# A decoder layer on one core: scores inside the recurrence from streamed per-head keys, and per-head values for the attention tail

## The reference

```python
# sLSTM stack (4 layers, 4 heads of 32), a scan over time
raw = wx_t + einsum('bhd,hdgo->bhgo', h, rk) + b
lfm = m + log_sigmoid(fr); mn = maximum(ir, lfm)
ig = exp(ir - mn); fg = exp(lfm - mn)
cn = fg * c + ig * tanh(zr); nn = fg * n + ig
hn = sigmoid(og) * cn / nn
# cross-attention, 16 heads of 64, context ctx_768 of 6404 x 96
q = (x @ Wq), k = (context @ Wk), v = (context @ Wv), split by head
attn = softmax(q @ k.T / sqrt(64)); out = (attn @ v) @ Wo + bo
# experts: top-1 routing with capacity, relu MLP 128 -> 512 -> 128
```

## Time and profile before

| | us |
|---|---|
| median of three runs | 4382.3 (4378.4 to 4395.1) |
| the profiled execution | 4380.9 |
| its span, first to last instruction | 4379.1 |
| plain chunks (320 steps) | 768.4 |
| 64 steps before the first tile | 181.8 |
| 832 steps with a tile | 2172.0 |
| tail, 816 tiles | 1026.0 |
| TensorE busy, of the span | 3756.0 (86%) |
| VectorE, ScalarE, GpSimd busy | 3519.7, 2778.4, 1036.2 |

### The profile page before, as it was taken

How to read it: one execution, slowest core, us unless ns; L and a number is a source line. 1 busy time by engine, 2 the same in 40 slices (tenths; PEclk the granted TensorE clock), 3 DMA queues, 4 the chain that set the end, 5 groups by cost and what they waited for, 6 DMA issues and landing times. The chain is left out here.

```text
span 4379.1 us, 103876 instructions
## 1 busy us (share of the span) xinstructions
PE 3756.0 (86%) x37640; PEld 2172.9 (50%) x37640; DVE 3519.7 (80%) x15928; ACT 2778.4 (63%) x8992; POOL 1036.2 (24%) x1218
## 2 busy tenths in 40 slices
PE   4666666459999999999999999999969999999997
PEld 3433334335445444544544544454426666666666
DVE  7777777688888888888888888888668787887875
ACT  4555555435666666666666666666717778877784
POOL 1000000000000000000000000000018888888883
PEclk6555555558999999999999999999969999999999
DMA  3111111000000000000000000000031221221100
GB/s 89 36 42 38 40 43 35 8 4 2 2 5 2 2 4 3 3 4 3 2 2 4 2 2 2 3 2 2 3 90 24 47 47 26 46 47 39 33 9 25
DMA packets 62974, 90.36 MB, mean 21 GB/s; under 512 B 11095, under 2 KB 58007, under 8 KB 59351
## 3 DMA queue, kind: packets, MB, share of 16 engines
q1 hardware_dynamic: 59282, 79.35, 7.3%
q10 hardware_dynamic: 3176, 4.36, 0.4%
HBM read 53.63 MB, written 28.83 MB: 19 GB/s over the span
## 5 line engine op out<-in xcount | busy, mean ns | idle before, releaser
L1214 PEld LDWEIGHTS G<-st,rec_w 128*128 128x128 f16 x19456 | 605.5, 99 | 961.3 <-DVE st L1385 926.5
L1214 PE MATMUL G<-st,rec_w 128*128 128x1 f16 x19456 | 683.0, 165 | 407.4 <-DVE st L1385 390.4
L1644 POOL TENSOR_TENSOR plt<-pft,pht 128x512 f16<-128x512 f32 x765 | 865.5, 1159 | 213.4 <-ACT pft L1639 110.5
L1166 PE MATMUL OA<-pf,vals 128*97 128x512 f32 (+1 forms) x1632 | 849.1, 601 | 0.6
L1089 ACT ACTIVATE st<-hb 32x16 f16<-32x16 f32 x1216 | 259.0, 213 | 703.0 <-DVE hb L1380 702.4
L130 DVE TENSOR_REDUCE mx<-MT 128x1 f32<-128x512 f32 (+1 forms) x832 | 531.7, 665 | 101.2 <-PE MT L1693 92.1
L1069 ACT ACTIVATE pf<-SC,ln_prob 128x512 f32<-128x512 f32 (+1 forms) x816 | 560.5, 687 | 20.6
L130 DVE TENSOR_REDUCE mx<-MB 128x1 f32<-128x512 f32 (+1 forms) x832 | 537.5, 660 | 37.7 <-PE MB L122 22.8
L1639 ACT ACTIVATE pft<-ST,ln_prob 128x512 f32<-128x512 f32 (+1 forms) x816 | 536.5, 684 | 36.0 <-PE ST L1715 30.9
L1637 ACT ACTIVATE pht<-ST,ln_prob 128x512 f16<-128x512 f32 x510 | 350.4, 687 | 241.8 <-PE ST L1715 235.7
L1080 ACT ACTIVATE tf<-G 32x16 f32<-32x16 f32 x1216 | 211.8, 174 | 384.6 <-PE G L1214 356.9
(11 more groups left out here) (354 smaller groups left out, 6774.2 us busy)
## 6 DMA issues: line engine op xcount, KB each, us to landing
kc<-scr_k SPq DMA_DIRECT2D x32, 816.0 KB, 13.1
scr_k<-k_hl SPq DMA_DIRECT2D x192, 128.0 KB, 1.7
k<-scr_k SPq DMA_DIRECT2D x16, 816.0 KB, 6.7
w<-in_L_ffn_W SPq DMA_DIRECT2D x16, 256.0 KB, 4.5
xin<-x SPq DMA_DIRECT2D x38, 48.0 KB, 1.8
scr_k<-k_hl SPq DMA_DIRECT2D x16, 96.0 KB, 1.6
rnat<-in_L_attn_rker SPq DMA_DIRECT2D x3, 256.0 KB, 13.8
up_w<-in_L_attn_ff_up SPq DMA_DIRECT2D x1, 672.0 KB
```

The source lines that it names most:

```text
L1166: pe.matmul(OA[0:at.DC + 1, :], at.vals[0:rows, i, :], pf[0:rows, tile % 2, :], start=(i == 0), stop=(i == KT - 1)).then_inc(pv_done, 1)
L1214: mm = pe.matmul(g[:, t, c:c + 1], rec_w[:, c, :], st[:, c:c + 1], start=False, stop=(c == C - 1), skip_group_check=True)
L1644: return eng.tensor_tensor(pl[0:k, t % NP_, :], pf[0:k, t % NP_, :], ph[0:k, t % NP_, :], ALU.subtract)
```

## The change

**Scores in tiled steps** use the same per-head form as the tail. Per tile and head two matmuls of 128 columns, eight in all, take the place of three of 512. Their keys no longer lie in SBUF: SP loads groups of four tiles by four heads from `scr_k` into a ring of three (`kc_in`: high and low part stacked to 128 rows; `k2_in`: high part and the row of ones), three DMAs a group, 208 groups. A group's buffer is refilled when the last tile of the group three before is done; loads that would fall on t = 15 to 19 are put off to t = 20. The queries for it (`pe_head_queries`, four matmuls with `wq_d`) are made three steps after the queries for the maxima, which remain; ScalarE copies them in two halves and VectorE takes the residue two steps later.

**Plain chunks** now also compute the values V = context times Wv by head, 102 pieces of one tile by eight heads, each again three matmuls of 512 columns, a copy and a residue. Pieces have 21 positions in a chunk; stores of up to four tiles by eight heads (1 MB) go to `scr_v`. The positions 22 and 24 of the weight preparation become 24 and 26. The split of `vals_c` is gone.

**The tail** loads `vc`, the per-head values, from `scr_v` and uses 129 and 65 columns instead of 193 and 97; the output is then multiplied by `wo_sb`. Loads of values for head g + 2 wait for the last product of head g.

Tensors used only in the plain chunks are freed after them; the two rings take their place, and two tensors of the setup share memory with `pf`.

```diff
-def pe_scores(pe, at, bank, j, unit, k):
-    keys = slice(j * P, j * P + k)
-    pe.matmul(bank[0:k, :], at.keys_l[:, keys], at.qh[0:DC, unit, :], start=True, stop=False)
-    pe.matmul(bank[0:k, :], at.keys_h[0:DC, keys], at.ql[:, unit, :], start=False, stop=False)
-    return pe.matmul(bank[0:k, :], at.keys_h[:, keys], at.qh[:, unit, :], start=False, stop=True)
+def pe_scores(pe, at, bank, j, unit, kept, k):
+    first = j % at.GROUP * P
+    for i in range(at.HEADS_A_UNIT):
+        cols = slice(i * P, (i + 1) * P)
+        pe.matmul(bank[0:k, cols], at.kc_in[:, kept, i, first:first + k], at.qd_in[:, unit, cols], start=(i == 0), stop=False,
+                  skip_group_check=True)
+        mm = pe.matmul(bank[0:k, cols], at.k2_in[:, kept, i, first:first + k], at.q2_in[:, unit, cols], start=False,
+                       stop=True, skip_group_check=True)
+    return mm
...
+def pe_head_queries(pe, at, bank, unit):
+    for i in range(at.HEADS_A_UNIT):
+        mm = pe.matmul(bank[:, i * P:(i + 1) * P], at.wq_d[:, unit * at.HEADS_A_UNIT + i, :], at.xat[:, :], start=True, stop=True)
+    return mm
...
+    T_NO_LOAD = range(15, 20)
+        self.head_queries = {s + 3: v for s, v in self.queries.items()}
-        for s in self.queries:
+        for s in self.head_queries:
             special[s + 2] = special.get(s + 2, 0.0) + 0.7
...
+        for g in range(self.groups):
+            s = last_tile[g - at.GROUPS_KEPT] + 1 if g >= at.GROUPS_KEPT else 0
+            if s % chunk_steps in self.T_NO_LOAD:
+                s += self.T_NO_LOAD.stop - s % chunk_steps
...
 class WeightsByHead:
-    PLACES = (3, 5, 6, 22, 24)
+    PLACES = (3, 5, 6, 24, 26)
-class KeysByHead:
-    PLACES = (0, 2, 4, 7, 8, 11, 12, 15, 18, 19, 21)
+class ByHead:
+    PLACES = (0, 1, 2, 4, 7, 8, 11, 12, 13, 14, 15, 16, 18, 19, 20, 21, 23, 25, 27, 28, 31)
+    TILES_A_STORE = 4
...
+                                sp.dma_start(at.kc_in[0:at.DHEAD, b, :, 0:a1 - a0], hi).then_inc(d_group[b], 16)
+                                sp.dma_start(at.kc_in[at.DHEAD:P, b, :, 0:a1 - a0], low).then_inc(d_group[b], 16)
+                                sp.dma_start(at.k2_in[0:at.DHEAD, b, :, 0:a1 - a0], hi).then_inc(d_group[b], 16)
...
+                                    rows, cols = slice(j * P, (j + 1) * P), slice(half * 512, (half + 1) * 512)
+                                    out = SC[i % 2][:, :]
+                                    pe.matmul(out, at.keys_l[:, rows], at.wv_h[:, cols], start=True, stop=False)
+                                    pe.matmul(out, at.keys_h[0:at.DC, rows], at.wv_l[:, cols], start=False, stop=False)
+                                    pe.matmul(out, at.keys_h[0:at.DC, rows], at.wv_h[:, cols], start=False,
+                                              stop=True).then_inc(k_full, 1)
...
-                       at.vals_c[0:k, j, 0:DC + 1], start=False, stop=(j == KT - 1), skip_group_check=True)
+                       vc[0:k, (t // KT) % 2, j, 0:DHEAD + 1], start=False, stop=(j == KT - 1), skip_group_check=True)
...
+                    sp.wait_ge(pv_done, KT * (g + 1))
+                    load_values(g + 2)
```

More of the change, by code:

```diff
@@ L42 @@
     HEADS_A_UNIT = 4
+    GROUP, GROUPS_KEPT = 4, 3
     C_SCALE = 2.0 ** 4
@@ new lines, in __init__ @@
+        self.values = [(j0 // self.TILES_A_STORE, half, j, j == min(j0 + self.TILES_A_STORE, at.KT) - 1)
+                       for j0 in range(0, at.KT, self.TILES_A_STORE) for half in range(2)
+                       for j in range(j0, min(j0 + self.TILES_A_STORE, at.KT))]
+        self.n_keys, self.total = len(self.keys), len(self.keys) + len(self.values)
+        self.v_stores = 2 * -(-at.KT // self.TILES_A_STORE)
+        places = [c * chunk_steps + p for c in range(chunks) for p in self.PLACES]
@@ L341, in slstm_stage, with in_chunk @@
+        assert self.total <= len(places)
+        self.at_step = {s: i for i, s in enumerate(places[:self.total])}
+    def in_chunk(self, chunk, late):
+        return [i for s, i in self.at_step.items()
+                if s // self.chunk_steps == chunk and (s % self.chunk_steps >= self.T_STORE) == late]
+def slstm_stage(nc, x, w, ctx_in, wa, scratch_in, scratch_out, dims, at, first_row, xa_out, keys_out, values_out, ones_out):
     S, D, L, H, K, UP = dims
```

294 lines of the change are left out of this document (191 added, 103 removed).

## The result

The changed kernel takes 4364.4 us (median of 10 runs, 4351.1 to 4370.4) against 4391.8 us for the kernel before (10 runs, 4378.4 to 4395.2): a ratio of 0.9938 [0.9924, 0.9952], 0.6% faster. The forecast was 4334 us, 1.1% under the profiled 4380.9. So the direction was right, and the gain was 27 us where 47 were forecast. The forecast took 4360 us as its bound for a gain that can be told from none, and 4364.4 lies above it; with ten runs of each kernel even this gain is clear of the noise. Of the 30 us between 4334 and 4364, 11 come from the start of the sum: the profiled 4380.9 was 11 us under the median that the kernel before has over 10 runs.

What follows compares the result with a forecast made beforehand. Plain chunks were taken as bound by the recurrence chain, tiled steps by chain or TensorE, the tail by TensorE. From the profiled 4380.9 us, +56 plain, -18 tiled and -85 tail gave 4334 us; own range 4305 to 4365.

Steps and rivals of the forecast that it cites:

- two thirds: Tail: the share of the 131 us from narrower value matmuls expected to arrive, since engines wait for each other: -85 us.
- the 90 us read off: Tail: VectorE waited 91 us for maxima's score matmuls, so beyond about 90 to 118 us of gain VectorE is last.
- Rival B: Tail: VectorE and GpSimd take over at once, only -40 us there, total time 4379 us; chance 0.20.
- t = 27: Plain chunks, a gate step: piece 0.7 us late, wq_d activations behind its copy 0.7 us more; 1.4 us a chunk.
- t = 16: Plain chunks: copy and scaling of vals exceed ScalarE's free 0.7 us, and the piece waits for SC; 0.8 us a chunk.
- A buffer is wanted again five steps after its last piece: Plain chunks, stores of values: reuse comes after 11.5 us at the earliest, against 6 or 14 us a store; nothing taken.
- Forecast -18: Tiled steps: scores -40 us, head queries +18 us, more ScalarE copies +4 us; together -18, bounds -50 and +15.
- A: Tail keeps the full gain and plain pieces hide better: -125 and +35, -10 in the middle, 4281 us; chance 0.13.
- E: Weight load and matmul pairs have a floor, so neither scores nor values shorten: 4459 us; chance 0.02.
- D: Tiled steps: key loads come late, 0.5 us each, total time 4438 us; chance 0.05.
- C: Tiled steps: the clock falls, 0.8 us a step, 83 us with one step in eight, 4417 us; chance 0.10.
- What "would show it": Expected trace signs: plain chunks some 82.5 us, over 584 chain waits, eight score matmuls 0.45 us, tail some 941 us.

Runs made afterwards that it cites:

- after: The profiled execution of the changed kernel, nothing further edited: 4370.4 us; tiled stretch 2168.8 us, tail 969.9 us.
- experiment 12: Changed kernel with four key buffers, scaling and wq_d activations moved, later head queries, second maximum behind the scores: 4339.2 us, ratio to before 0.9882.
- experiment 11: Changed kernel with four buffers in place of two for pieces of keys on their way to memory: 4357.9 us, plain stretch 804.0 us.
- the pad: Changed kernel with one more 512-column fp16 matmul ahead of each tile's eight score matmuls in the tiled stretch: 4405.6 us, ratio to before 1.0031.
- both256: Changed kernel with VectorE's maxima and GpSimd's low parts in the tail both cut to 256 of 512 columns: 4271.7 us, tail 890.4 us.
- experiment 1: The kernel before the change, unedited, measured again for a second profile: 4387.7 us median, tiled stretch 2177.1 us with 99 us at half clock.
- mx256: Changed kernel with VectorE reducing only 256 of 512 columns of the tail's maxima: 4325.1 us, tail 948.4 us.

## Why the prediction was wrong in size

**The tail: the step that failed.** "Engines with little slack wait for each other, so I take two thirds, **-85 us**." The columns did fall by 0.16 us a tile (four of 129 columns now 0.23 us, four of 65 0.12 us, where the earlier trace rows have 0.33 and 0.18), and 131 us is about what they are worth, since 890 us came out once VectorE and GpSimd were relieved. But only 56 us, 43% of it, arrived; the term was 29 us too large. Waits between engines were the right mechanism; the two thirds were a guess without a working, and the 90 us read off were taken as a point up to which VectorE would follow for free. That number is a sum of gaps, and says nothing of where they lie.

Three things made the loss of 75 us larger than the 46 taken. First, the matmuls that VectorE needs come in pairs with two banks. In tiles with one maximum the median fell by the full 0.155 us (1.16 to 1.01 us), in those with two, 195 of 815, by 0.03 (1.38 to 1.35). Means weigh the rare long waits too: 1.392 to 1.382 us with two maxima, 1.253 to 1.168 with one (390 tiles), 1.155 to 1.064 with none (230 tiles). So the pairs lose 29 of the 75 us, tiles with one maximum 29 and those with none 16. Second, 10 of these 16 are the last head, where GpSimd was last already before the change. Third, VectorE's low parts grow beside GpSimd's, so that their busy times are not separate budgets: 51 times 0.6 us, 30 us of VectorE's time in after, where it was 20 before. How much of the 75 us that makes was not taken apart. Rival B had the right mechanism (short bursts, two banks) at too low a value, -40; the measured value lies between the two.

**The plain chunks: right kind, 14 us too much.** 42.3 us against 56, and 81.5 and 80.6 us a chunk against 82.5. Term by term (us a chunk, forecast, then measured as the difference of the mean steps): t = 27 1.4 and 0.69 (the wq_d activations stand behind the copy there and were counted with 0.7, but the step without them was to cost 0.7 as well); t = 28 0.9 and 0.63, of which 0.17 went when experiment 12 moved the activations away; t = 31 0.45 and 0.15; t = 16, which shows in the step at 17, 0.8 and 1.15 with keys (0.43 of it the wait for a store that experiment 11 removes) or 0.67 with values; the convolution at t = 24 0.7 and 0.60; t = 15 0.4 and 0.3; t = 22 back 0.6, measured 0.22 to 0.35. So the largest miss is at t = 27, 0.7 us a chunk for activations that cost next to nothing there, then t = 28 and 31, 0.6 us together; against them stand 0.35 us too little at t = 17 with keys. "Gate steps t = 27 and 28 near 3.7 and 3.2 us" came out as 2.99 and 2.93. "A buffer is wanted again five steps after its last piece" was for values and held (no wait for a store of values). For keys the question wasn't asked: their two buffers come round every second step at adjacent places, and experiment 11 shows that 6.7 us of the 42.3 were this wait for a DMA of 1.7 us, in a place where only a wait for VectorE was priced. So the sum was 14 us too large although it left out a term of 7.

**The tiled steps.** Forecast -18 together with the 64 steps ahead; at equal half-clock time -17 to -19, and +5 in the 64 steps (the first two head queries fall at half clock, and the steps around them grew by 1.2 and 3.8 us, where 1.1 each was taken), so -12 to -14. The scores gave 0.16 us a step in place of 0.197, since the second record of a tile's values starts 25 ns later; the pad shows some 228 steps that pay, which were counted at 248. The head queries cost 0.65 to 0.9 us each within the 1.1 taken.

**Setup and start of the tail** differ by -2.5 and +2.1 us; not looked into.

**The rivals.** A's tail (full gain) is what both256 reaches, and E and D are out by measurement. C's premise, that the clock would fall in many more steps, is not seen: the clock is 0.97 to 0.98 in the stretch in every profile, and the estimate of experiment 1 has 105 us at half clock before and 104 after. What "would show it" came out: 608 waits for the chain in place of 584, 0.46 us for eight matmuls, clock 0.97, and more waits of TensorE in the tail; only 970 us stood in place of 941. That 4364.4 lies just inside the forecast's own range of 4305 to 4365 is partly luck: the tail fell short by 29 us, and the plain chunks cost 14 us less than forecast.

## What to carry to other kernels

Columns taken from the engine that is busiest are worth their full price only where no engine around it is within that price of it in the same tile: look at the tightest repeating place (here a pair of maxima on two banks) and at stretches with another balance (here the last head), not at the sum of the other engines' idle time. When two engines hold a stage in turn, relief of one is cut short by the other: here 21.5 and 41.8 us alone, 79.5 together. Work placed in an engine's "free" step must stand ahead of that step's waits in its queue; behind them the free time is gone and all its cost is left. And where the same code differs by 20 us between runs, profile each kernel more than once before a stage's difference is read.

## What the runs showed that was not expected

- A VectorE subtraction of two SBUF operands (128x512, fp32) took 0.68 to 0.69 us on average where no GpSimd subtraction was under way when it began, 1.288 us in after, where one always was, and 1.51 us in mx256. Why it is longer in mx256 than in after was not looked into.
- A tile's fp32 values show as two records. The second starts 0.457 us after the first when a 128-column matmul stands ahead of the first, and 0.432 us when a 512-column one does; with and without DMA traffic alike. Why was not tried.
- The same code at the same stage differed by up to 20 us between runs, by 0.34 us for each us that the clock spent at half speed; one profile of each kernel would have put the tiled stretch at -0.6 in place of about -18 us.
- 156 MB of key groups streamed at 76 GB/s beside a TensorE that is 91% busy cost nothing that can be measured; the waits for 128 KB stores of keys cost 6.7 us in all.
